# Probabilities times V for two steps at a time in a transformer block on one Trainium2 core

## What is computed

```python
q, k, v = x @ Wq + bq, x @ Wk + bk, x @ Wv + bv          # per head
scores = where(causal, q @ k.T / sqrt(64), -inf)
out = concat_heads(softmax(scores) @ v) @ Wo + bo
x = layernorm(x + out)                                     # norm of attention
xn = layernorm(x) * gamma + beta
w, idx = top_k(softmax(xn @ router_w.T / 1.5), 2)          # router
y = sum over the two experts of w * (silu(xn @ W1[e]) @ W2[e])
x = layernorm(x + y)
```

## Time and profile before

| | us |
|---|---|
| median of 3 runs (1371.1 to 1372.15) | 1372.0 |
| the profiled execution | 1359.07 |
| its span, first to last instruction | 1357.2 |
| TensorE busy in the span | 1292.0 |
| VectorE busy | 1105.1 |
| ScalarE busy | 1103.4 |
| GpSimd busy | 761.0 |

### The profile page before, as it was taken

The page is one execution under the profiler, slowest core; times in us unless marked ns, Lnnn a source line. Parts: engine busy times, 40 slices in busy tenths (PEclk is TensorE's granted clock), DMA queues, the critical chain, the costliest instruction groups (busy, mean ns, idle before and its releaser), DMA issues.

```text
span 1357.2 us, 36506 instructions
## 1 busy us (share of the span) xinstructions
PE 1292.0 (95%) x11106; PEld 1130.0 (83%) x11106; DVE 1105.1 (81%) x5169; ACT 1103.4 (81%) x3513; POOL 761.0 (56%) x1365
## 2 busy tenths in 40 slices
PE   7999999999999999999999999999986798989997
PEld 6888888888888888888888888888866788988893
DVE  6888888888888888888888888888975676767747
ACT  7999999999899998898989999888864566666647
POOL 2446666565565666655556566665556554545545
PEclk9999999999999999999999999999998899999999
DMA  5000000000000000000000000000335576666649
GB/s 201 21 21 29 33 34 31 31 29 14 14 14 14 13 18 17 16 16 14 14 14 14 14 13 18 17 16 15 138 91 143 157 210 189 204 197 186 199 128 338
DMA packets 58864, 98.21 MB, mean 72 GB/s; under 512 B 9376, under 2 KB 36131, under 8 KB 58416
## 3 DMA queue, kind: packets, MB, share of 16 engines
q1 hardware_dynamic: 49024, 78.67, 18.5%
q0 software_dynamic: 8640, 17.13, 3.7%
q10 hardware_dynamic: 1008, 0.08, 0.1%
HBM read 65.85 MB, written 30.91 MB: 71 GB/s over the span
## 4 chain that ended last, share of the span: by engine, by line
PE 82%; ACT 6%; issue 5%; DVE 3%; another core or an unknown queue 2%; POOL 1%; DMA 1%; SPq 0%; ACTq 0%; POOLq 0%; DVEq 0%
PE ps_b L1224 13%; PE ps_a L1190 13%; PE ps_s L1231 12%; PE ps_s L1212 9%; PE ps_f L1190 7%; PE ps_f L1262 7%; PE ps_s L1190 6%; PE ps_s L1215 4%; PE ps_b L1444 3%; PE ps_a L1444 2%; PE ps_s L1516 2%; DVE f_y L1141 2%; ACT qk L658 1%; ACT qk L659 1%
## 5 line engine op out<-in xcount | busy, mean ns | idle before, releaser
L669 ACT ACTIVATE f_y<-f_y,neg_max 128x256 f32<-128x256 f32 x512 | 255.5, 499 | 59.9 <-DVE neg_max L926 59.6
L926 DVE CUSTOM_DVE_ANT_0 f_y<-ps_s,mask 128x256 f32<-128x256 f32 x512 | 215.0, 420 | 35.3 <-PE ps_s L1215 27.2
L568 POOL CAST ot_hi<-f_y 128x512 fp32r<-128x512 f32 x128 | 80.3, 628 | 257.8 <-ACT f_y L702 244.3
L634 POOL DMA_INDIRECT y_tok<-f_y,m_dest x142 | 143.5, 1011 | 137.1 <-DVE m_dest L1096 93.0
L1231 PE MATMUL ps_s<-ident,f_y 128*128 128x128 f32 x1536 | 200.9, 274 | 0.0
L940 DVE TENSOR_SCALAR f_y<-f_y,inv_sums 128x256 f32<-128x256 f32 x512 | 192.7, 376 | 9.1
L672 ACT ACTIVATE f_y<-f_y,neg_max 128x128 f32<-128x128 f32 x512 | 198.6, 388 | 0.0
L1224 PE MATMUL ps_b<-pt,f_y 128*64 128x256 f32 (+1 forms) x2048 | 194.7, 332 | 1.7 <-issue 1.4
L1212 PE MATMUL ps_s<-qk 64*128 64x256 f32 x1024 | 173.4, 414 | 8.1 <-ACT pt L716 2.7
L1224 PEld LDWEIGHTS ps_b<-pt,f_y 128*64 128x64 f32 x2048 | 130.6, 136 | 51.4 <-issue 2.9
L1231 PEld LDWEIGHTS ps_s<-ident,f_y 128*128 128x128 f32 x1536 | 172.7, 143 | 0.3 <-issue 0.3
(11 more groups left out here) (219 smaller groups left out, 3564.2 us busy)
## 6 DMA issues: line engine op xcount, KB each, us to landing
m_w<-w_split SPq DMA_DIRECT2D x71, 512.0 KB
m_x<-queue SPq DMA_DIRECT2D x71, 133.0 KB
f_y<-y_tok SPq DMA_DIRECT2D x32, 256.0 KB, 6.4
queue<-empty SPq DMA_DIRECT2D x8, 532.0 KB
x_raw<-in_x SPq DMA_DIRECT2D x32, 128.0 KB, 2.1
w_split<-f_y SPq DMA_DIRECT2D x8, 512.0 KB, 2.6
out_x<-f_y SPq DMA_DIRECT2D x16, 256.0 KB, 7.1
y_tok<-f_y,m_dest POOLq DMA_INDIRECT x142
```

Source lines behind the costliest of these rows:

```text
L634: pool.indirect_dma_start(y_tok, bass.IndirectOffsetOnAxis(ap=m_dest[:, j % (2 * YBUFS), i:i + 1], axis=0), m_y[:, j % YBUFS, i, :], None, ...
L669: act.activation(row[:, 0:2 * P], row[:, 0:2 * P], ACT.Exp, scale=-1.0, bias=neg_max[:, pair, h, 0:1], accum_out=sums[:, d % 2, pair, h, 0:1])
L926: dve.tensor_tensor_reduce(out=row[:, 0:2 * P], in0=ps_s[:, pair, h, 0:2 * P], in1=mask[:].rearrange("p a b -> p (a b)"), scale=-1.0, scal ...
```

## The change

- The product with V is taken for two steps at once, in steps 1 and 3 alone: `outputs(d - 3)` into `ps_b` and `outputs(d - 2)` into `ps_f`, each a step older than before for the first of the two. `pt` gets a second buffer. ScalarE copies the first result after the exponentials and the second at the step's end.
- V is projected in step 0 alone: the second half of the sequence before, two tiles one behind the other into `ps_b` and `ps_f`, and at the step's end the first half of this sequence in the same way. VectorE evacuates those in `ps_b`, ScalarE those in `ps_f`.
- The output projection stands wholly in step 2, ahead of and behind the transposes; the next input is transposed in step 2 and loaded in step 1. The router's logits stand ahead of both groups of transposes in step 0, and what VectorE makes of them follows its maxima; the ranks stay in step 2 and are also taken up right after the maxima. In step 1 the router's top two is cut into pieces between the scalings of `normalise`.
- In step 3 ScalarE and VectorE exchange the two copies into `pt`; `variance` stands behind the first two maxima, and `statistics` directly behind `residual`. GpSimd takes two roundings and two rests in steps 0 and 2, and `xb` in step 1. The split of the experts' weights moves to step 3.

The diff (`...` where lines are left out):

```diff
-        pt = sb("pt", [P, 2, 2, 3 * P])
+        pt = sb("pt", [P, 2, 2, 2, 3 * P])
...
+        def outputs_at(s):
+
+            return ps_b if s % 2 == 0 or s == LAST - 1 else ps_f
...
-                if q == 0 and 1 <= n < SEQS - 1:
+                if q == 1 and 1 <= n < SEQS - 1:
...
-                if q <= 2 and n in MID:
-                    round_outputs(d - 1)
+                if q in (0, 2) and n in MID:
+                    round_outputs(d - 4)
                     pool.wait_ge(scores_ready, d * 2 + 1)
-                    rest_of_outputs(d - 1)
-                if q == 0 and n in MID:
-                    residual_input(n)
+                    rest_of_outputs(d - 4)
+                    round_outputs(d - 3)
+                    rest_of_outputs(d - 3)
                 if q == 0 and n - 1 in LATE:
                     slots(n - 1)
                     send_tokens(n - 1, 0)
-                if q == 2 and 1 <= n <= E:
-                    rest_of_w1(n - 1)
+                if q == 1 and n in MID:
+                    pool.wait_ge(scores_ready, d * 2 + 1)
+                    residual_input(n)
                 if q == 1 and n - 1 in LATE:
                     send_tokens(n - 1, 1)
-                if q == 2:
-                    round_outputs(d)
-                    rest_of_first_outputs(d)
+                if q == 3 and 2 <= n <= E + 1:
+                    pool.wait_ge(scores_ready, d * 2 + 1)
...
+            for s in range(LAST - 4, LAST - 2):
+                round_outputs(s)
+                rest_of_outputs(s)
+            slots(SEQS - 1)
+            send_tokens(SEQS - 1, 0)
+            for s in range(LAST - 2, LAST):
+                round_outputs(s)
+                rest_of_outputs(s)
+            residual_input(SEQS)
...
-                if q == (1 if n >= 1 else 2) and n + 1 < SEQS:
+                if q == 2 and n + 1 < SEQS:
                     round_input(n)
-                if d == LAST - 1 or q == 2:
-                    copy_outputs(d)
+                if q == 0 and n in MID:
+                    evacuate_second_v(n * 4, 1)
+                if d == LAST - 1:
+                    copy_outputs(d - 3)
                 if d < LAST:
                     for h in range(2):
                         exponentials(d, 1, h)
-                if q == 2 and n in MID:
-                    copy_projection(n)
+                if d >= 3 and q in (1, 3) and d < LAST - 1:
+                    copy_outputs(d - 3)
+                if d == LAST - 1:
+                    copy_outputs(d - 2)
                 if d == LAST - 1:
                     first_pt(d)
                     act.wait_ge(zt_ready, n)
...
-                if d >= 2 and q == 0:
-                    copy_outputs(d)
                 if d + 1 < LAST:
                     evacuate_qk(d + 1, 0)
-                if 1 <= d < LAST - 1:
+                if 1 <= d < LAST - 1 and q < 3:
                     first_pt(d)
+                if q == 2 and n in MID:
+                    copy_projection(n)
                 if d + 1 < LAST:
                     evacuate_qk(d + 1, 1)
-                if 2 <= d < LAST - 1 and q in (1, 3):
-                    copy_outputs(d)
-                if q == 1 and 1 <= n <= E:
+                if q == 3 and d < LAST - 1:
+                    act.wait_ge(pt_second_ready, d)
+                    act.activation(pt[:, (d - 1) % 2, 1], ps_s[:, 1, :, 0:3 * P], ACT.Copy).then_inc(pt_second_done, 1)
+                if 3 <= d < LAST - 1 and q in (1, 3):
+                    copy_outputs(d - 2)
+                if q == 2 and n == SEQS - 1:
+                    evacuate_second_v(n * 4 + 4, 1)
+                if q == 3 and 1 <= n <= E:
                     e = n - 1
                     act.wait_ge(w1_loaded, 16)
...
+                    if q == 0 and n in MID:
+                        evacuate_first_v(n * 4 - 1, 1)
+                    if q == 0 and n in LATE:
+                        router_difference(n)
+                    if q == 2 and n in LATE:
+                        places(n)
+                    if q == 1 and n in LATE:
+                        reciprocals(d, 0)
+                        find_top(n)
+                        scale(d, 0, 0)
+                        find_index(n)
+                        scale(d, 0, 1)
+                        find_gates(n)
+                        reciprocals(d, 1)
+                        find_chosen(n)
+                        scale(d, 1, 0)
+                        find_any(n)
+                        scale(d, 1, 1)
                     else:
-                        rest_of_xt(n + 2, (n + 1) % 2)
-                if n in LATE:
-                    router(n, q)
-                    if n in (SEQS - 3, SEQS - 2):
-                        keep_counts(n, q)
...
-                if d == LAST - 1 or (q == 1 and n in MID):
+                if d == LAST - 1 or (q in (0, 2) and n >= 1):
                     second_pt(d)
-                if d < LAST:
+                if d < LAST and not (q == 1 and n in LATE):
                     normalise(d, 1)
                 if q == 2 and n in MID:
                     residual(n)
-                    second_pt(d)
                     statistics(n)
-                if 1 <= d < LAST - 1 and (q in (0, 3) or n == 0):
+                if q == 3 and d < LAST - 1:
+                    dve.wait_ge(pt_first_ready, d)
+                    dve.tensor_copy(pt[:, (d - 1) % 2, 0], ps_s[:, 0, :, 0:3 * P]).then_inc(pt_first_done, 1)
+                elif 1 <= d < LAST - 1 and (q == 1 or n == 0):
...
-                if q == 0 and n in LATE:
-                    router_difference(n)
+                if q == 0 and n in MID:
+                    evacuate_first_v(n * 4 + 1, 0)
...
+            def second_half_of_v(n):
+                pe.wait_ge(ot_done, n * QUADS + 1)
+                if n == 0:
+                    pe.wait_ge(attn_w_lo, 6)
+                v_projection(n % 2, 1, 0, ps_b)
+                pe.wait_ge(ot_done, n * QUADS + 2)
+                v_projection(n % 2, 1, 1, ps_f)
+
+            def outputs(s):
+                pe.wait_ge(pt_first_done, s + 1)
+                pe.wait_ge(pt_second_done, s + 1)
+                for pair in range(2):
+                    ins = attention_output(s, pair)
+                ins.then_inc(o_ready, 1)
...
+                if q == 0:
+                    if n >= 1:
+                        second_half_of_v(n - 1)
                     else:
-                        pe.wait_ge(v_done, n * 4)
-                    v_projection(n % 2, 0, 0)
-                if q == 1 and n == 0:
-                    pe.wait_ge(v_done, 2)
-                    pe.wait_ge(wo_loaded, 16)
-                    pe.wait_ge(bv_wide_done, 1)
-                    product(ps_f[:, 0:D], [(bv_wide[:, c, :], wo_sb[:, c, :]) for c in range(PAIRS)]).then_inc(bo_ready, 1)
-                if q == (1 if n >= 1 else 2) and n + 1 < SEQS:
+                        first_half_of_v(0)
+                    first_pair()
+                    if n in LATE:
+                        pe.wait_ge(xnt_done, n - 1)
+                        pe.wait_ge(max_done, d * 4 + 4)
+                        router_logits(n)
...
+                if q == 1:
+                    if n >= 1:
+                        pe.wait_ge(v_first_done, n * 2 + 1)
+                        pe.wait_ge(v_second_done, n * 2)
+                        outputs(d - 3)
+                        pe.wait_ge(v_second_done, n * 2 + 1)
+                        outputs(d - 2)
...
+                        pe.wait_ge(attn_w_lo, 5)
+                    first_pair()
+                    first_transposes(d)
+                    second_transposes()
...
+                if q == 2:
+                    if n < SEQS - 1:
+                        next_input(n)
+                    else:
+                        pe.wait_ge(ot_done, n * QUADS - 1)
+                        v_projection(n % 2, 1, 0, ps_b)
+                    first_pair()
+                    if n >= 1:
+                        output_projection(n, 0)
+                    if n in LATE:
+                        pe.wait_ge(r_diff_done, n - 1)
+                        pe.wait_ge(chosen_any_done, n - 1)
+                        pe.wait_ge(max_done, d * 4 + 4)
+                        ranks(n)
+                    first_transposes(d)
+                    if n in LATE:
+                        pe.wait_ge(ranks_done, n - 1)
+                    second_transposes()
+                    if n >= 1:
+                        output_projection(n, 1)
+                    second_pair()
+                    if n >= 1:
+                        transpose_projection(n)
+                    if n == SEQS - 1:
+                        pe.wait_ge(v_first_done, n * 2 + 2)
+                        v_projection(n % 2, 1, 1, ps_b)
...
+                if q == 3:
+                    if n == SEQS - 1:
+                        pe.wait_ge(v_second_done, n * 2 + 2)
+                    else:
```

(24 more changed lines are left out.)

367 lines of the change are left out of this document (155 added, 212 removed).

## The result

The changed kernel takes 1381.95 us (median of 20 runs, 1372.06 to 1384.73), the kernel before 1370.15 in the same comparison (20 runs, 1364.59 to 1372.93): a ratio of 1.0084 with a 95% interval of 1.0073 to 1.0095. It is 11.8 us slower. The forecast was 1376, so 4 to 4.5 us slower, in a range of 1361 to 1387, with slower as the likeliest sign.

A forecast was written before the change was run, and what follows sets the result against it. TensorE bounds the kernel. A sequence's work of 29.78 us, waits of 1.09 and contention of 0.15 gave 31.02 in place of 30.87, 30 times: +4.5 on the median of 1372.0, so 1376 us, range 1361 to 1387.

The forecast's parts named there:

- the second pair's scores in step 0: TensorE waits 0.38 us there for ScalarE's copy of the second transposes, 0.49 with the slower block behind it.
- those in step 2: The second pair's scores in step 2 wait for ScalarE's last evacuation, 0.35 us, a wait moved from step 3.
- z's transposes: In step 3 TensorE waits 0.25 us for z from GpSimd, ready at 5.33 where TensorE arrives at 5.08.
- The two products: Two products with V side by side in steps 1 and 3 take 2.73 us, with one changeover paid once.
- The rival that they pay twice: Two products into two banks pay two changeovers, 10 us more, 1386 us; chance 0.10.
- the twelve transposes: TensorE's twelve transposes in a step take 1.23 us.
- step 3's scores: TensorE's block of scores in step 3 takes 1.53 us.
- the 29.78 of the sum: TensorE's work in the four steps of a sequence without the waits, against 30.87 us before.
- The contention: VectorE and GpSimd holding each other up, mainly roundings beside scalings in steps 1 and 3, costs 0.15 us a sequence.
- The start and the last two sequences: The ends of the attention stage change by 0, ±2 us.
- the expert stage: The 71 expert steps are untouched by the change.
- VectorE falls behind: Rival: VectorE's full step 0 makes it late, delaying maxima, exponentials and TensorE, 0.6 us a sequence, 1390 us; chance 0.20.

The follow-up runs named there:

- e4: Changed kernel with the six projections of the next first pair put between the two products with V in steps 1 and 3; ratio 1.0138 to the kernel before.
- e5: Changed kernel with GpSimd's first rounding of steps 0 and 2 held back until the step's first scores are there; ratio 1.0057 to the kernel before.
- e10: e1 with GpSimd's four indirect DMAs of the tokens put ahead of the residual input in step 1; 1388.38 us in one run.
- e2_var: Changed kernel with the variance taken ahead of the maxima in step 3; ratio 1.0042 to the kernel before.
- e7: e1 with step 0's logits behind the first transposes and the second pair's projections ahead of the second transposes; ratio 1.0047 to the kernel before.
- e8: Changed kernel with four edits together, those of e7 (V's tile, logits), e2_var (variance) and e9 (input's transposes); 1366.97 us, ratio 0.9978 to the kernel before.
- e12: Changed kernel with step 0's logits behind the first transposes and second pair's projections ahead of the second transposes, V's tile unmoved; ratio 1.0109 to the kernel before.
- e1: Changed kernel with one of step 0's V tiles moved to the end of the step 3 before it; ratio 1.0052 to the kernel before.
- e9: Changed kernel with the next input's transposes moved from the start of step 2 to the end of step 1; ratio 1.0053 to the kernel before.
- e11_all_v: e8 with the evacuation of V's first tile in step 0 moved from VectorE to ScalarE; ratio 0.9984 to the kernel before.

## Why the prediction was right, and where it was off

**The sign and the mechanism.** Merging the products and V's tiles saves TensorE's work, and waits that the change moves or makes eat it. The size did not come out: 11.8 us lost, where 4.5 was the forecast; the time lies in the range because the range was wide. All three waits stand where the prediction put them, released by what it named: the second pair's scores in step 0 by ScalarE's copy (1.13 measured, 1.14 forecast), those in step 2 by the evacuation (0.99, forecast 1.0), z's transposes in step 3 behind GpSimd. The steps are 8.09, 7.18, 8.22 and 7.68, forecast 8.0, 7.1, 8.15 and 7.6.

**The two products** took 2.75, forecast 2.73 from a changeover paid once. The rival that they pay twice (1386) is out, by this row and by e4, whose 0.44 a sequence is the merge's worth. The time came out nearer to that rival's 1386 than to 1376, which shows how little a time alone says of its cause.

**Terms that were mis-sized.** The blocks, all a little: the twelve transposes 1.27, not 1.23; step 3's scores 1.64, not 1.53; z's transposes 0.27, not 0.21. The four steps' work is 0.44 above the 29.78 of the sum, 0.25 of it in step 3. A part of that is a fourth wait which the forecast hasn't: in step 3 the second pair's scores (529.17) start 0.51 behind ScalarE's evacuation (528.66), the distance of the earlier trace rows (0.52), and the block behind them takes 0.86, not 0.77. Against the 0.44 stand two terms that were too large. The wait for z is 0.11 in place of 0.25: z was ready at 5.30 (forecast 5.33), since VectorE was on time (maximum at 0.97, not 1.09) but the chain from the variance took 3.21, not 3.13, and TensorE arrived at 5.20, not 5.08. The contention is 0 in place of 0.15: e5 took it away and gained nothing. With the two waits for ScalarE as forecast (0.35 and 0.49) that is 31.17 in place of 31.02, and 28 to 30 times 0.15 is 4.2 to 4.5 us by which the forecast of the sequences was low. It would have been lower still without luck: the two terms that were too large hid 0.29 of the 0.44. The start and the last two sequences gave 0.8, and the expert stage took 1.3, where 0 stood; the medians lie another 1.4 to 2.4 us apart beyond the 9.4 of the two spans, which no profile explains.

**VectorE against GpSimd.** The fear for VectorE was right in kind: e10 has a scaling of 0.57 in place of 0.28 beside a two-input operation of GpSimd (the residual input). The prediction took the scaling of 0.34 in the earlier trace rows as a sign that two-input operations do no harm. But the one beside it (L501) works on two values in each partition only. Beside a long one, the rest of an expert's weights, the kernel before has a slow scaling in each of the eight sequences in which they meet (0.68 to 0.70):

```profile
211.19 1.29 POOL L551 TENSOR_TENSOR f_y<-f_y 128x512 fp32r<-128x512 f32 x1
...
211.94 0.68 DVE L940 TENSOR_SCALAR f_y<-f_y,inv_sums 128x256 f32<-128x256 f32 x1
```

The Trainium skill, "SBUF — State Buffer", section "SBUF: two separate sides", says that the two engines share a port pair as an exclusive lock, held for the whole instruction. These rows agree with it; the one beside L501 (528.71 to 529.43) does not. What the prediction missed beyond that was that the copy behind the scalings in step 1 has 0.3 of slack. In e2_var a slow scaling did reach the path.

**VectorE falls behind** was given 0.20 and did not happen in the changed kernel: its first maximum starts at 0.97 in every step. It did happen in e7, e8 and e12 (1.31 to 1.41), as soon as step 0 was made shorter or the logits later. The full list of step 0 was the right thing to fear, one edit too early.

**What the sum does not say.** A reader could draw from it, and the expectation of e1 did, that the wait of 0.49 in step 0 is there to be had back. e1 removed it and gained nothing, since two more limits stood behind it, the logits' bank (0.41) and ScalarE's chain (7.11). A sum of waits prices what is there; it doesn't price their removal.

## What to carry to other kernels

Where three engines pass banks to each other in a loop, a wait that one sees is only the latest of several; before taking it away, work out when the next one behind it would release, on every engine, and edit them together (a sequence 0.02 longer for the cover alone, 0.43 shorter on average for four edits). Where nothing else stood behind, in e9, one edit gained its 0.15 alone. A move of blocks on the busiest engine should be read by what it uncovers: a tile that looks like plain work was the cover of a copy. And compare variants by the distance between repeated starts within a trace: in most kernels here its mean repeated to 0.02 us, while the same kernel differed by 10 us between chips. But look at every repetition before trusting a median or a part: in e2 and e8 eight of 28 sequences were 0.4 longer, and that took most of the gain of one and a fifth of the gain of the other.

## What the runs showed of the hardware

A ScalarE instruction that had its inputs started late around the packets of an indirect DMA. In e1_cover and e5_cast the evacuation of step 1 started 1.64 to 1.73 us behind the start of the last indirect DMA in the 28 sequences from 3 to 30, whether that was at 3.95 or 4.07 of the step. In sequences 3 to 29 of the changed kernel and of e2_var, where the DMA was issued at 3.33 to 3.68, it started at 5.44, unheld. Sequence 2 has no such DMA, and there it started at 5.44 in e1_cover and e5_cast too. In e10_send it was the copy ahead that came late, 1.86 to 1.95 behind the DMA's start, so the distance is no constant. In e11_all_v it cost 0.36 in the sequence shown, on the path. What is held, the instruction, its semaphore or a memory access, no run tells. The hold in e11_all_v began ahead of the packets (546.35, packets from 546.50), and other ScalarE instructions started on time beside such packets (549.14 in the changed kernel, with packets from 549.0 to 549.2).

Changing the shape of the array costs at both edges, and the runs give the parts: a product between other kinds takes 1.45, the first of two 1.35, the second 1.40, so 0.10 go with the way out, 0.05 with the way in and 1.30 are the product. The block ahead of it takes 0.09 more, the transposes behind it 0.06 more. Step 1 of e4_split has one such product more alone than the changed kernel: 0.30 in all. In step 3 it was 0.15, since there part of it fell into the wait for z.
